# A windowed-attention block in fp32: parameters behind the first rows, second transposes in another bank pair, output transposes beside those of the probabilities

## The reference

```python
h = roll(ln(x, ln1_g, ln1_b), (-4, -4))            # axes 1, 2
win = window_partition(h, 8)                       # (512, 64, 64)
q, k, v = split(win @ qkv_w + qkv_b, 3)            # 4 heads of 16
attn = q @ k.T * 16 ** -0.5 + bias[rel_pos] + shift_mask
out = softmax(attn) @ v @ proj_w + proj_b
x = x + roll(window_reverse(out), (4, 4))
return x + gelu(ln(x, ln2_g, ln2_b) @ fc1_w + fc1_b) @ fc2_w + fc2_b
```

## Time and profile before

| what | us |
|---|---|
| median of three runs (501.3 to 502.0) | 501.9 |
| the profiled execution | 501.78 |
| its span | 499.7 |
| TensorE busy / DVE / ACT / POOL | 469.1 / 356.0 / 365.2 / 337.3 |
| mean granted TensorE clock | 0.979 |
| stretches: to 93.12 / to 324.08 (six groups) / to 352 / to the end | 93.1 / 231.0 / 27.9 / 147.7 |

### The profile page before, as it was taken

The page is one execution under the profiler, slowest core; times in us unless marked ns, Lnnn a source line. Parts: engine busy times, 40 slices in busy tenths (PEclk is TensorE's granted clock), DMA queues, the critical chain, the costliest instruction groups (busy, mean ns, idle before and its releaser), DMA issues.

```text
span 499.7 us, 21543 instructions
## 1 busy us (share of the span) xinstructions
PE 469.1 (94%) x9634; PEld 352.5 (71%) x9634; DVE 356.0 (71%) x528; ACT 365.2 (73%) x523; POOL 337.3 (67%) x347
## 2 busy tenths in 40 slices
PE   4566999999999999999999999998999999999996
PEld 2443777877877877778787787787667666766665
DVE  3755789698698788788788788794655776774542
ACT  1325798978887887887987988886776686677653
POOL 4333997966966966966966956977238669669400
PEclk9777999999999999999999999999999999999999
DMA  8204421411321231231101101100003312321333
GB/s 166 63 1 112 97 50 34 98 40 31 83 59 35 68 75 36 53 83 41 43 5 47 34 13 45 29 19 4 3 3 87 86 23 66 85 49 41 86 82 90
DMA packets 10251, 27.05 MB, mean 54 GB/s; under 512 B 3520, under 2 KB 3520, under 8 KB 8352
## 3 DMA queue, kind: packets, MB, share of 16 engines
q1 hardware_dynamic: 9968, 25.48, 21.6%
q0 software_dynamic: 128, 0.13, 0.1%
q10 hardware_dynamic: 64, 0.07, 0.0%
HBM read 9.15 MB, written 8.39 MB: 35 GB/s over the span
## 4 chain that ended last, share of the span: by engine, by line
PE 84%; DVE 6%; DMA 4%; SPq 2%; ACT 2%; issue 1%; POOL 1%; ACTq 0%; POOLq 0%; DVEq 0%
PE work L826 26%; PE outs L826 17%; PE scores L826 12%; PE trans L924 12%; PE trans L826 7%; PE scores L964 4%; PE work L841 3%; PE outs L952 3%; DMA x<-in_x 3%; DMA kX<-kT 1%; SPq L304 1%; DVE stat_sq L511 1%; DVE probs L569 1%; DVE x L617 1%; DVE negmax L575 1%
## 5 line engine op out<-in xcount | busy, mean ns | idle before, releaser
L456 POOL TENSOR_TENSOR probs<-probs,negmax 128x1024 f32<-128x1024 f32 x64 | 121.9, 1905 | 42.4 <-DVE negmax L575 41.6
L569 DVE TENSOR_TENSOR probs<-scores,bias 128x1024 f32<-128x1024 f32 x64 | 78.1, 1221 | 40.5 <-PE scores L826 40.4
L764 ACT ACTIVATE probsT<-trans 128x1024 f32<-128x1024 f32 x64 | 65.5, 1024 | 36.5 <-PE trans L924 36.1
L575 DVE TENSOR_REDUCE negmax<-probs 128x16 f32<-128x1024 f32 x64 | 78.1, 1220 | 2.2
L826 PE MATMUL scores<-kX,qT 32*64 32x128 f32 x2048 | 71.8, 276 | 7.9 <-DVE probs L569 4.9
L826 PEld LDWEIGHTS work<-params,probs 128*64 128x64 f32 x2048 | 62.2, 138 | 23.5 <-issue 14.4
L826 PEld LDWEIGHTS outs<-vX,probsT 128*64 128x64 f32 x2048 | 64.9, 138 | 18.5 <-issue 14.7
L826 PE MATMUL outs<-vX,probsT 128*64 128x34 f32 x2048 | 72.1, 225 | 1.6 <-issue 0.9
L924 PE MATMUL trans<-ident,probs 128*128 128x128 f32 x512 | 70.5, 281 | 0.0
L826 PEld LDWEIGHTS scores<-kX,qT 32*64 32x64 f32 x2048 | 56.0, 133 | 20.4 <-issue 11.5
L375 POOL TENSOR_TENSOR xn<-x,stat_mean 128x256 f32<-128x256 f32 (+1 forms) x92 | 69.1, 775 | 0.2
(11 more groups left out here) (78 smaller groups left out, 697.0 us busy)
## 6 DMA issues: line engine op xcount, KB each, us to landing
kX<-kT SPq DMA_DIRECT2D x124, 64.0 KB, 2.0
x<-in_x SPq DMA_DIRECT2D x28, 224.0 KB
out<-x SPq DMA_DIRECT2D x28, 224.0 KB
x<-in_x SPq DMA_DIRECT2D x8, 112.0 KB
x<-in_x SPq DMA_DIRECT2D x28, 32.0 KB
out<-x SPq DMA_DIRECT2D x28, 32.0 KB
out<-x SPq DMA_DIRECT2D x16, 56.0 KB
params<-in_params SPq DMA_DIRECT2D x1, 741.5 KB, 11.2
```

The lines of the kernel that those rows point to most:

```text
L456: nc.gpsimd.tensor_tensor(e, e, top, ALU.add).then_inc(shifted, 1)
L569: nc.vector.tensor_tensor(e[:, :].rearrange("q (u a m) -> q a u m", u=2, a=2), scores[:, :].rearrange("q (a u m) -> q a u m", a=2, u=2), b ...
L575: nc.vector.tensor_reduce(negmax[n % 4][:, :], e[:, :].rearrange("q (a m) -> q a m", m=N), AXX, ALU.max, negate=True).then_inc(negmax_read ...
L764: nc.scalar.activation(probsT[n % 2][:, :], trans[:, :], ACT.Copy)\
```

## The change

SP waits for both halves of the first rows before it issues the parameters and load(1). TensorE warms up with five matmuls, sums the biases ahead of the first transposes, and puts the second half of x's first transposes into the banks of `trans`, without a wait for ACT's copy of the first half. ACT copies the summed biases before it takes both halves; DVE scales the q/k/v weights between the second and third piece of x, and sums group 1 after the first keys. In each step, `transpose_o` and its copy on ACT come right behind the transposes of the probabilities and ahead of the tasks at n + 0.5, and there is a new place n + 0.25 between `weigh` and the transposes. The two XT change places in time (3.25 and 3.5), V moves to 6.25 and 8.25, the second Y to 7.5. LayerNorm steps move by up to two steps; the first sum of group 2 goes from step 2 to step 1, and the first half of the y bias from step 4 to step 0. On DVE the sums come ahead of the Y additions, on POOL the y bias and the shift ahead of root and mean, on ACT the squares ahead of the tasks. `warm(0)` issues nothing.

```diff
--- before.py
+++ after.py
@@ -68,11 +68,11 @@
 def group_tasks(first, last):
-    tasks = [(1, "QK", 2), (2.0, "V", 1), (2.5, "QK", 3), (4.0, "V", 2), (6.0, "V", 3)]
+    tasks = [(1.0, "QK", 2), (2.0, "V", 1), (2.5, "QK", 3), (4.0, "V", 2), (6.25, "V", 3)]
     if not last:
-        tasks += [(3, "XT", 0), (3.5, "XT", 1), (5.5, "QK", GI), (7, "QK", GI + 1), (8.0, "V", GI)]
+        tasks += [(3.5, "XT", 0), (3.25, "XT", 1), (5.5, "QK", GI), (7.0, "QK", GI + 1), (8.25, "V", GI)]
     if not first:
-        tasks += [(4.5, "Y", 0), (6.5, "Y", 1)]
+        tasks += [(4.5, "Y", 0), (7.5, "Y", 1)]
     return sorted(tasks)
@@ -96,20 +96,19 @@
...
-LN_STEPS = {"sum": (-19, -18, -17, -16), "mean": (-16,), "centre": (-15, -14, -13, -12),
-            "square": (-14, -13, -12, -11), "square_sum": (-13, -12, -11, -10), "seed": (-9,),
-            "root": (-8,), "scale": (-8, -7, -6, -5)}
+LN_STEPS = {"sum": (-19, -18, -16, -16), "mean": (-15,), "centre": (-14, -14, -13, -12),
+            "square": (-13, -13, -12, -11), "square_sum": (-12, -11, -10, -10), "seed": (-10,),
+            "root": (-10,), "scale": (-10, -8, -7, -6)}
 LN_STEPS_EARLY = {
-    1: {"sum": (-1, -1, -1, -1), "mean": (-1,), "centre": (-1, -1, -1, -1),
-        "square": (0, 0, 0, 0), "square_sum": (0, 0, 0, 0), "seed": (1,), "root": (2,),
-        "scale": (2, 2, 2, 3)},
-    2: {"sum": (2, 2, 3, 3), "mean": (3,), "centre": (4, 4, 5, 5), "square": (5, 5, 6, 6),
-        "square_sum": (6, 6, 7, 7), "seed": (7,), "root": (8,), "scale": (8, 9, 10, 11)}}
+    1: {"sum": (-1, -1, -1, -1), "mean": (-1,), "centre": (0, 0, 1, 1), "square": (0, 1, 1, 1),
+        "square_sum": (1, 1, 1, 1), "seed": (1,), "root": (2,), "scale": (2, 2, 2, 2)},
+    2: {"sum": (1, 2, 3, 3), "mean": (3,), "centre": (4, 4, 4, 5), "square": (5, 5, 5, 5),
+        "square_sum": (6, 6, 7, 7), "seed": (7,), "root": (8,), "scale": (8, 10, 10, 10)}}
 LN_AHEAD = GROUPS + 2
-Y_BIAS_STEPS = (4, 6)
+Y_BIAS_STEPS = (0, 6)
...
@@ -308,12 +307,14 @@
...
                 for dst, src in rows_of(x_d, 0, 2 * WIN * half, 2 * WIN * (half + 1), (UPPER,)):
                     sp.dma_start(dst, src).then_inc(x0_loaded[half], 16)
+            for half in range(2):
+                sp.wait_ge(x0_loaded[half], 16 * GI)
             sp.dma_start(params[:, :], params_d).then_inc(params_in, 16)
             load(1)
...
             for n in range(-1, PAIRS):
                 g, s = divmod(n, STEPS)
-                for kind, of, i in tasks_at(n) + tasks_at(n + 0.5):
+                for kind, of, i in tasks_at(n) + tasks_at(n + 0.25) + tasks_at(n + 0.5):
                     if kind == "QK" and (of, i) != (0, 0):
                         spread_keys(of, i)
...
@@ -479,13 +480,13 @@
...
                 for group, i in ln_at("centre", n):
                     centre_piece(group, i)
+                if n % STEPS in Y_BIAS_STEPS:
+                    add_y_bias(n // STEPS, Y_BIAS_STEPS.index(n % STEPS))
+                shift_pair(n)
                 for group, _ in ln_at("root", n):
                     root(group)
                 for group, _ in ln_at("mean", n):
                     mean(group)
-                shift_pair(n)
-                if n % STEPS in Y_BIAS_STEPS:
-                    add_y_bias(n // STEPS, Y_BIAS_STEPS.index(n % STEPS))
                 for group, j in ln_at("scale", n):
                     scale(group, j)
...
@@ -543,14 +544,16 @@
...
                 square_sum(j, j)
-            for j in range(PIECES):
-                scale_rows(0, j)
-
+            scale_rows(0, 0)
+            scale_rows(0, 1)
             dve.wait_ge(params_in, 16)
             for t in range(3):
...
                                                ALU.mult)
             last.then_inc(weights_scaled, 1)
+            scale_rows(0, 2)
+            scale_rows(0, 3)
+
             r = rpb[:, :].rearrange("q (h m) -> q h m", h=HEADS).unsqueeze(2)\
                 .to_broadcast([P, HEADS, 2, N])
...
@@ -617,8 +620,6 @@
...
                                                    ALU.add)
                 done.then_inc(y_added, 1)
-
-            norm(-1)
             dve.wait_ge(params_ready, 4)
...
@@ -630,6 +631,7 @@
...
             nc.vector.tensor_scalar(w1[:, :], w1raw[:, :], gain[:, 1:2], None, ALU.mult)\
               .then_inc(w1_ready, 1)
+            norm(-1)
             for n in range(PAIRS + TAIL):
                 if n < PAIRS:
...
@@ -637,14 +639,14 @@
...
                 for group, i in ln_at("square_sum", n):
                     square_sum(PIECES * group + i, i)
-                for k2 in (0.5, 1):
-                    for kind, of, i in tasks_at(n - k2):
-                        if kind == "Y":
-                            add_y(of, i)
                 for group, i in ln_at("sum", n):
                     if group >= GROUPS:
                         dve.wait_ge(y_added, COUNT["Y", group - GROUPS, 1])
                     sum_piece(group, i)
+                for k2 in (0.5, 0.75, 1):
+                    for kind, of, i in tasks_at(n - k2):
+                        if kind == "Y":
+                            add_y(of, i)
             for kind, of, i in tasks_at(PAIRS + TAIL - 0.5):
                 add_y(of, i)
@@ -704,7 +706,8 @@
...
                     dst = xT[of % 2][:, :].rearrange("q (i p c r) -> q p c i r", p=2, r=WIN, c=WIN)
                     nc.scalar.activation(dst[:, i],
-                                         work2[:, :].rearrange("q (c i r) -> q c i r", c=WIN, r=WIN),
+                                         (trans if (of, i) == (0, 1) else work2)[:, :]
+                                         .rearrange("q (c i r) -> q c i r", c=WIN, r=WIN),
                                          ACT.Copy).then_inc(xT_copied, 1)
                 elif kind == "QK":
...
@@ -734,8 +737,6 @@
...
             first_seed(0)
             first_seed(1)
-            for kind, of, i in tasks_at(-1)[:2]:
-                take(kind, of, i)
             act.wait_ge(biases_summed, 1)
             nc.scalar.activation(bqkv[:, 1:2], scores[:, 1:2], ACT.Copy).then_inc(params_ready, 1)
...
@@ -750,9 +751,10 @@
...
             act.wait_ge(params_ready, 3)
-            for kind, of, i in tasks_at(-1)[2:]:
+            for kind, of, i in tasks_at(-1):
                 take(kind, of, i)
-            squares_of(-1)
+                if (kind, i) == ("QK", 0):
+                    squares_of(-1)
             def exp(n):
...
@@ -775,20 +777,23 @@
...
             for n in range(PAIRS):
+                squares_of(n)
                 for kind, of, i in tasks_at(n):
                     if kind != "Y": take(kind, of, i)
                 for group, _ in ln_at("seed", n):
                     seed(group)
-                squares_of(n)
+                for kind, of, i in tasks_at(n + 0.25):
+                    if kind != "Y":
+                        take(kind, of, i)
                 if 0 <= n - TR < PAIRS:
                     copy_trans(n - TR)
+                if 0 <= n - OUT < PAIRS:
+                    copy_oT(n - OUT)
                 for kind, of, i in tasks_at(n + 0.5):
                     if kind != "Y":
...
                 if n < PAIRS:
                     exp(n)
-                if 0 <= n - OUT < PAIRS:
-                    copy_oT(n - OUT)
             def copy_xT2(s):
...
@@ -829,7 +834,7 @@
...
             def fill(kind, of, i):
-                if (kind, of, i) in BEFORE:
+                if (kind, of, i) in BEFORE and (kind, of, i) != ("XT", 0, 1):
                     copied(*BEFORE[kind, of, i])
                     if BEFORE[kind, of, i] == ("QK", 0, 0):
...
@@ -838,7 +843,8 @@
...
                         for k in range(4):
                             jj = 8 * i + 4 * half + k
-                            done = nc.tensor.transpose(work[half][:, k * P:(k + 1) * P],
+                            to = trans[:, half * BANK:] if (of, i) == (0, 1) else work[half]
+                            done = nc.tensor.transpose(to[:, k * P:(k + 1) * P],
                                                        xn[of % 2][:, jj * P:(jj + 1) * P], ident[:, :])
                 elif kind == "QK":
@@ -874,9 +880,9 @@
...
                 done.then_inc(work_ready[kind], 1)
-            def warm(n):
+            def warm(n, columns=BANK):
                 for _ in range(n):
-                    mm(trans[:, 0:BANK], ident[:, :], kX[0][:, 0, :])
+                    mm(trans[:, 0:columns], ident[:, :], kX[0][:, 0, 0:columns])
             def sum_biases():
...
@@ -967,11 +973,13 @@
             pe.wait_ge(pool_ready, 2)
             pe.wait_ge(zeroed, 2)
-            warm(6)
+            warm(5)
+            sum_biases()
+            warm(0)
             for kind, of, i in tasks_at(-1):
                 fill(kind, of, i)
-                if (kind, i) == ("XT", 0):
-                    sum_biases()
+                if kind == "XT":
+                    warm(0, P)
                 if (kind, i) == ("XT", 1):
```

(6 more changed lines are left out.)

## The result

The changed kernel takes 506.85 us (median of 22 runs, 503.19 to 514.47) beside 503.55 us for the kernel before (22 runs beside it): ratio 1.0067, 95% interval 1.0043 to 1.0090. It is slower by 2.2 to 4.5 us. All ratios are of runs in the fast state; three of the changed kernel's 22 (510.75 to 514.47) were in the slow one, and the other 19 have a median of 506.50. The profiled execution took 503.68 us for a span of 501.7 (before: 501.78 and 499.7), at a mean granted clock of 0.984.

The account below looks back on a forecast made before the run. TensorE's own stream was taken to bound 93 to 324 us, a chain of waits the start. 501.78 - 2.0 (start, first group) + 3.9 (six groups) - 0.3 (end) = 503.4 us; 8-in-10 range 498.0 to 507.0.

Parts of the forecast that it names:

- The sign: Whole kernel: slower than before; slower by over 0.2% was given a chance of 0.45, faster 0.35.
- load(2) wait: First group: DVE's sum, moved to step 1, waits for load(2); pair 3's scores 3.7 us later, loss of 3.0 taken.
- the middle: Six groups: 0.95 us saved, next keys, x transposes and V wait added; +0.65 a group, +3.9 in all.
- the end: Last group: fewer changes of shape, Y's second half moved to where TensorE stands 0.94 us anyway; -0.3 us.
- Rows and parameters: Start: rows land at 8.2, parameters at 15.7, 7.0 us after issue; q/k product gains 5.0 us.
- Rivals 4 and 5: Start: 4, rows land as late as before, 505 us, chance 0.10; 5, parameters take 11.2 us again, 506.5 to 507, 0.08.
- Rival 1, the clock: Start: early biases keep TensorE at 2.4 GHz, transposes -1.9 and q/k product -2.2 us; 499.3 us, chance 0.23.
- some is regained: First group: group 1's transposes stand later and their stalls vanish, so 3.0 of 3.7 us is lost, bounds 1.5 and 3.7.
- the x transposes: Middle: the second half waits for ACT's copy of the first to free the bank; 0.3 us a group.
- the V wait: Middle: the V product behind the second half of the x transposes waits 0.23 us a group.
- The keys: Middle: next group's key copy, no longer covered by Y's second half, stalls TensorE 0.84 us, plus 0.25 for long landings.
- (c): Middle: LayerNorm steps, POOL's order and ACT's earlier o copy cost nothing; up to 0.5 us a group if cover fails.

Follow-up runs that it names:

- rows_first: The kernel before with only SP's wait: parameters and load(1) issued behind the first rows; 501.44 us, ratio 0.9961.
- after: The changed kernel itself, with the whole change against the kernel before; 506.85 us, ratio 1.0067.
- four: Changed kernel with group 2's first sum in step 2, next keys' product at 5.25, Y additions ahead of sums, later groups' first sum one step later; 495.01 us.
- sum_step2: The changed kernel with the first sum of group 2 back in step 2; 500.31 us, ratio 0.9960.
- start_only: The kernel before with only the start part: SP's wait, five warm-ups, early bias sums, second bank pair, matching ACT and DVE order; 497.88 us, ratio 0.9884.
- four_keys_late: The kernel four with the next group's first q/k product at 5.5, as in the changed kernel; 498.67 us, ratio 0.9913.
- y1_back: The changed kernel with the second Y in step 6 again (6.5 for 7.5); 506.90 us, ratio 1.0071.
- load2_early: The changed kernel with load(2) issued right behind load(1), group 2's first sum staying in step 1; 501.69 us, ratio 0.9973.
- order_only: The kernel before with only the o transposes and ACT's o copy right behind the transposes of the probabilities; 507.31 us, ratio 1.0086.

## Why the prediction was right, and where not

**The sign** came out as forecast: slower, by the load(2) wait and the middle against the start. The profiled execution, 503.68 us, is 0.3 from the 503.4 of the sum, and that is luck: against the forecast the start gained 2.0 more, the first group lost 2.1 more, the six groups lost 0.7 less and the end 0.9 more. By the medians the loss is 3.3 us, twice the forecast's 1.6 (a ratio of 1.0032, below the interval from 1.0043); 506.85 lies inside the range (to 507.0) by a hair, and beyond the forecast's own (502.5 to 505.5).

**Rows and parameters.** Rows at 8.54 (forecast 8.2). The parameters landed in 4.6 us after their issue at 9.24, not in 7.0, so biases began at 13.90, and the wait for them, which I put on the path, is off it: TensorE waits for the normalized rows. The forecast of the first transposes (17.8 at the earliest) still came out (18.10), since that bound was the rows'. The q/k product at 23.33 lies within 22.9 to 25.1. That it does is in part luck: the parameters came 1.8 sooner than the forecast's 15.7, and the rows, not they, set the time. Rivals 4 and 5 fell: rows_first shows the rows sooner, and nobody waits long for the parameters. The rule from the Trainium skill behind rival 4 (DMA: Bandwidth & Descriptors, Queues, rings and completion order) is not contradicted by that: it is on the order in which descriptors are consumed, and the section adds that a later one may finish its write first, so that "could not overtake" went further than it does. The transfer that had been late was POOL's, on another queue, and of order within one queue these runs show nothing.

**Rival 1, the clock,** came in part. The clock did fall near 18 us, though TensorE had been busy with the bias sums until 16.6; in before it fell near 18.1 (0.55), 3.8 us behind the warm-up's end at 14.3, not the 4.5 that I read. In after's profiled execution the transposes still ran at a granted clock of 0.62 and 0.53; the q/k product ran at 2.4 GHz, in 1.96 us and not the 1.1 that I took, and the start gained 7.0 us at pair 0; nine of the experiments have the same code up to there, and in the profiles of seven of them pair 0 starts at 28.72 to 29.23, a gain of 4.8 to 5.3 (27.27 and 26.78 in the other two). Of the seven, `four` has the clock back at 26 us and sum_step2 only behind 42. So whether it is back by 22 us varies from execution to execution; start_only's median says 5.0.

**The load(2) wait.** Mechanism, place and time of the wait were right: DVE got the rows 13.66 us behind the second q/k product (43.73 - 30.07; forecast 14.0), pair 3 started 15.53 us behind it (forecast 15.8). The step that failed is "some is regained": I took 3.0 of 3.7, and it cost 4.3 by the trace and 5.0 by the medians. Nothing was regained. The stand of 5.14 us put TensorE at 1.2 GHz for the next step, 1.6 us more, which no term of the sum had, though the earlier trace rows had shown the clock fall during a pause. That is the part with the largest consequence: with the sum left in step 2 the change would have been faster than before (500.31 us).

**The middle.** The terms as written add up to +0.67 a group, not +0.65. Savings less the x transposes and the V wait were forecast at -0.95 + 0.3 + 0.23 = -0.42; 37.75 in `four` against 38.16 without stalls is -0.41. Only this net came out: in the group from 203.53 us the second x transposes start 0.46 us behind the o transposes (0.31 is the usual distance) and V 1.18 behind the scores (1.03), so that the two waits are 0.15 each, and the saving must have been smaller than 0.95 too. The keys were forecast at 0.84 and 0.25 for long landings; alone they cost 0.6 (four_keys_late against four). Path and distance were right (5.72 for 5.81, a wait of 0.68); the size net of the step is lower. What filled the gap is (c), the sum ahead of Y's addition on DVE, which I costed at nothing with "up to 0.5 a group if that cover fails". It failed: POOL, DVE and ACT had 6 to 8 us of slack a group, but DVE's slack is no cover for an instruction that waits for a transfer with others behind it. In after it cost 0.86 us in three groups (2.6 us on TensorE), a part of it in place of key waits. So +0.54 a group (39.03 against 38.49 in the mean) met the forecast with one term too large and one missing, which is luck again.

**The end** was forecast at -0.3 and gave +0.6 from pair 60 on. I had moved Y's second half to where TensorE stands anyway. That wait of 0.94 did go; but the product before it had been covered by the same Y, and now waits itself:

```profile
341.73 1.13 PE L831 MATMUL outs<-vX,probsT 128*64 128x34 f32 x32 [1.20 <-ACT probsT L766]
```

So Y's move gave nothing, and it is not what cost either: y1_back, with Y in its old step and the 0.94 back, takes as long from pair 60 to the end of the span (177.3 us in both, 176.8 before). Nor did the saved changes of shape show. All ten profiles of kernels with the changed order have this end, 177.3 to 177.4; which part of the order makes it was not tried.

**The rest between 1.9 and 3.3 us** is argued: with a start gain of 5.2 instead of 7.0, as in seven of those nine profiles, the profiled difference of 1.9 would be 3.7, near that of the medians. No run shows it.

## What to carry to other kernels

Slack of an engine is no cover for an instruction that can wait: before you move one forward, look at what lands when, and at what its queue holds behind it. An index of one step on an engine with 6 us of slack a group cost 4 to 5 us here, about as much as the whole start part had won. When a change has several parts, try each alone and the losers mended together: on the changed kernel, mending the keys or DVE's order alone brought nothing clear (507.2 and 505.0 us), since each wait hid a part of the other; with the sum of group 2 mended too, the two were worth 5 us together (495.0 beside the 500.3 of sum_step2).

## What was not expected of the hardware

The pause of TensorE ahead of pair 3 was paid twice: 5.14 us of waiting, and 1.2 GHz in the next step, 6.33 us instead of 4.76. With a pause of 0.93 us ahead of the same pair (load2_early) TensorE had 1.00 from 42 to 50 us.

In eleven of the fourteen profiles (not in order_only, sum_step2 and four_keys_late) TensorE also stops once or twice between two matmuls of one product, for nothing that the trace shows ("issue"), for example in start_only:

```profile
138.10 1.04 PE L828 MATMUL work<-params,oT 64*64 64x64 f32 x54
140.49 0.39 PE L828 MATMUL work<-params,oT 64*64 64x64 f32 x10 [1.35 <-issue]
```

It falls in the second and third group, from 0.32 to 1.35 us, and makes their times differ by about as much as the terms of this case. In each of the eleven the stop begins 0.1 to 1.3 us after a transfer on the queue that the page lists as `q8 instruction` has ended (here one from 137.66 to 139.00, the stop from 139.14). Such transfers come every few us without a stop as well; whether they cause it was not tried.
